# A fused stack of conditional layers on one core: shared weights at another byte remainder, and routed down products as six matmuls of 256 columns

## What is computed

```python
x = x + L0(x, cond_8)     # x @ W0[b].T + bias, W0[b] = sum over g of y[b, g] * weight[g] * mask
x = x + L1(x, cond_8)     # x @ (W_base + 2 * sum over e of w[b, e] * B[e] @ A[e]).T + b_base
x = x + L2(x, cond_8)     # two of 8 experts per sample, weighted by w_route, and one shared expert:
                          #   (gelu(x @ gate) * (x @ up)) @ down, inner width 512
x = x + L3(x, cond_8)     # one of 8 experts per sample: (silu(up) * gate) @ down with biases, inner width 256
```

## Time and profile before

| | |
|---|---|
| median of 3 runs | 135.24 us (135.14 to 135.24) |
| the profiled execution, its own time | 135.81 us |
| its span, first to last instruction | 134.0 us |
| mean granted TensorE clock | 0.996 |
| TensorE busy | 129.9 us, 97% |
| VectorE (DVE), ScalarE (ACT), GpSimd (POOL) busy | 101.7, 99.0, 75.2 us |

### The profile page before, as it was taken

How to read it: one execution, slowest core, us unless ns; L and a number is a source line. 1 busy time by engine, 2 the same in 40 slices (tenths; PEclk the granted TensorE clock), 3 DMA queues, 4 the chain that set the end, 5 groups by cost and what they waited for, 6 DMA issues and landing times.

```text
span 134.0 us, 3164 instructions
## 1 busy us (share of the span) xinstructions
PE 129.9 (97%) x866; PEld 118.9 (89%) x866; DVE 101.7 (76%) x201; ACT 99.0 (74%) x205; POOL 75.2 (56%) x89
## 2 busy tenths in 40 slices
PE   7999999999999999999999999999999999999990
PEld 5988888888888899999999999999999999999980
DVE  0589898797775777768877687877868677898791
ACT  3774699979946478777797777766767659989860
POOL 0228449979980027468496684963452634426770
PEclk9999999999999999999999999999999999999998
DMA  4999999999005955556765657756577465665224
GB/s 151 329 395 400 415 399 402 397 403 378 19 0 213 373 202 232 237 232 247 313 257 224 248 218 313 286 220 248 220 287 312 191 273 227 259 271 203 72 87 157
DMA packets 11489, 34.54 MB, mean 258 GB/s; under 512 B 1104, under 2 KB 2512, under 8 KB 11472
## 3 DMA queue, kind: packets, MB, share of 16 engines
q1 hardware_dynamic: 11184, 34.15, 65.0%
q10 hardware_dynamic: 288, 0.20, 0.5%
HBM read 12.32 MB, written 1.05 MB: 100 GB/s over the span
## 4 chain that ended last, share of the span: by engine, by line
PE 90%; DVE 3%; ACT 1%; POOL 1%; issue 1%; ACTq 0%; DVEq 0%; POOLq 0%
PE up L298 31%; PE acc L298 30%; PE gate L298 29%; DVE x_res L1003 1%; DVE h_pair L923 1%; DVE up L1012 1%; POOL x_lo L779 1%; POOL x_res L805 1%; ACT h_pair L636 0%; ACTq L224 0%; ACT h_act L689 0%; DVE h_pair L1035 0%; DVE acc L1028 0%; ACT h_pair L709 0%; DVE x_res L1044 0%
## 5 line engine op out<-in xcount | busy, mean ns | idle before, releaser
L773 POOL TENSOR_TENSOR dn_lo<-slabs,dn_hi 128x256 fp32r<-128x256 f32 x40 | 29.7, 742 | 39.6 <-ACT dn_hi L654 39.5
L630 ACT ACTIVATE h_act<-gate 128x512 f32<-128x512 f32 x48 | 28.8, 600 | 23.9 <-PE gate L298 22.6
L923 DVE TENSOR_TENSOR h_pair<-up,h_pair 128x512 fp32r<-128x512 f32 x55 | 37.5, 681 | 0.0
L933 DVE SCALAR_TENSOR_TENSOR up<-h_act,w_route,up 128x512 f32<-128x512 f32 x32 | 24.1, 754 | 15.0 <-PE up L298 14.4
L298 PE MATMUL gate<-x_hi,w_gu 128*128 128x256 f32 x160 | 34.3, 278 | 0.0
L298 PE MATMUL up<-x_hi,w_gu 128*128 128x256 f32 x158 | 33.4, 276 | 0.0
L636 ACT ACTIVATE h_pair<-up 128x512 fp32r<-128x512 f32 x55 | 32.8, 597 | 0.0
L298 PEld LDWEIGHTS gate<-x_hi,w_gu 128*128 128x128 f32 x160 | 27.3, 188 | 0.2
L298 PE MATMUL acc<-h_pair,dn_hi 128*128 128x512 f32 (+1 forms) x76 | 27.2, 373 | 0.0
L298 PEld LDWEIGHTS up<-x_hi,w_gu 128*128 128x128 f32 x158 | 26.8, 188 | 0.0
L298 PE MATMUL gate<-x_lo,w_gu 128*128 128x256 f32 x80 | 22.2, 277 | 0.0
(11 more groups left out here) (128 smaller groups left out, 205.1 us busy)
## 6 DMA issues: line engine op xcount, KB each, us to landing
w_gu<-slabs SPq DMA_DIRECT2D x40, 512.0 KB, 3.0
slabs<-slabs_moe SPq DMA_DIRECT2D x8, 768.0 KB, 13.1
slabs<-slabs_l SPq DMA_DIRECT2D x4, 768.0 KB, 8.5
sh_raw<-slabs_shared SPq DMA_DIRECT2D x2, 384.0 KB, 5.2
x_res<-x_rest SPq DMA_DIRECT2D x1, 768.0 KB, 6.9
outT<-x_res SPq DMA_DIRECT2D x6, 128.0 KB, 1.9
slabs<-second_in SPq DMA_DIRECT2D x1, 320.0 KB, 3.3
slabs<-third_in SPq DMA_DIRECT2D x1, 256.0 KB, 3.8
```

Source lines behind the costliest of these rows:

```text
L630: nc.scalar.activation(h_act[:, u % 2, :], gate_ps[u % 2][:], ACT.Gelu_apprx_tanh).then_inc(act_done, 1)
L773: nc.gpsimd.tensor_tensor(dn_lo[:, q % W_SLOTS, :], slab_cols(at, DOWN_AT, 256), dn_hi[:, q % W_SLOTS, :].bitcast(F32), ALU.subtract).then ...
L923: V.tensor_tensor(h_lo[:, u % H_SLOTS, :], h_of(u), h_hi[:, u % H_SLOTS, :].bitcast(F32), ALU.subtract).then_inc(h_lo_done, 1)
L933: ins = V.scalar_tensor_tensor(h_of(u), h_act[:, k, :], weight, h_of(u), ALU.mult, ALU.mult)
```

## The change

Two things are done. place_sh grows from 24 to 40 elements and place_w (16 elements) goes, so that sh_hi and sh_lo begin 64 bytes later, at remainder 416, and everything from w_gu on stays where it was. And `routed_down` calls `slab_down`: six matmuls of 256 columns that all add to the same 256 columns of acc; `add_halves` and its semaphore go, and `add_acc` takes its place with one addition.

```diff
-        place_sh = sb("place_sh", [P, 24])
+        place_sh = sb("place_sh", [P, 40])
         sh_hi = sb("sh_hi", [P, HALVES * SLAB], F32R)
         sh_lo = sb("sh_lo", [P, HALVES * SLAB], F32R)
-        place_w = sb("place_w", [P, 16])
         w_gu = sb("w_gu", [P, W_SLOTS, 2 * SLAB_GU], F32R)
...
-        d_out, half_added, last_half = sem("d_out"), sem("half_added"), sem("last_half")
+        d_out, last_half = sem("d_out"), sem("last_half")
...
                 if j == 0:
                     acc_bank_free(PAIRS + b)
-                hidden_split(R0 + q)
-                pe.wait_ge(wd_hi_done, q + 1)
-                pe.wait_ge(wd_lo_done, q + 1)
-                slot = (R0 + q) % H_SLOTS
-
-                def both(c, start, stop):
-                    w, h = slice(c * P, (c + 1) * P), slice(c * S, (c + 1) * S)
-                    return mm(acc(b, 512), dn_hi[:, q % W_SLOTS, w], h_pair[:, slot, :, h], start, stop)
-
-                def low(c):
-                    w, h = slice(c * P, (c + 1) * P), slice(c * S, (c + 1) * S)
-                    mm(acc(b, S), dn_lo[:, q % W_SLOTS, w], h_hi[:, slot, h], False, False)
-
-                both(0, j == 0, False)
-                low(0)
-                low(1)
-                both(1, False, j == 3).then_inc(down_done, 1)
-
+                slab_down(R0 + q, q, acc(b, S), j == 0, j == 3)
...
-            def add_halves(b, down):
-
-                at = slice(b * S, (b + 1) * S)
-                dve.wait_ge(down_done, down)
-                V.tensor_tensor(x_res[:, at], acc(b, 512)[:, S:2 * S], x_res[:, at], ALU.add).then_inc(half_added, 1)
-                dve.wait_ge(half_added, b + 1)
-                V.tensor_tensor(x_res[:, at], acc(b, S), x_res[:, at], ALU.add).then_inc(acc_read, 1)
-
...
-                        add_halves(b - 1, R0 + 4 * b)
+                        add_acc(b - 1, S, R0 + 4 * b)
...
-                    add_halves(B - 1, T0)
+                    add_acc(B - 1, S, T0)
```

## The result

The changed kernel takes 138.41 us (median of 6 runs, 137.48 to 138.64) against 135.24 for the kernel before (6 runs, 134.91 to 135.32). The profiled execution took 138.64 us with a span of 136.8. The forecast was 134.3, the range ended at 137.3.

The account below looks back on a forecast made before the run. TensorE, busy 97% of the span and never idle between 53 and 118 us, was taken as the bound. From 135.24 us, -0.86 and -0.11 (sum -0.97) gave 134.3 us; the range holding 8 in 10 was 134.1 to 137.3.

Parts of the forecast that it names:

- The narrow form saves 0.86 us: Routed stage: six narrow matmuls per down product bring 32 units from 2.067 to 2.040 us each, -0.86 us.
- The trace has the new form already: Last stage: it already runs six narrow matmuls through the same function, buffers and remainders, at 2.040 us per unit.
- The mixture of remainders costs 0.11 us: From 45.49 to 53.08 us, alternating remainders 352 and 416 cost TensorE 7.59 instead of 7.48 us; equal ones save 0.11.
- For even ones speaks the one sort of wide matmul at 416: Routed down products: the first wide matmul, 53.08 to 53.31 us, was taken as evidence that wide ones at 416 are even.
- The first rival: Shared stage: wide matmuls at 416 are uneven and cost 0.48 to 0.96 us, giving 134.8 to 135.2 us; chance 0.19.
- The sticking pace: From q = 2 to 127 us: some 650 narrow matmuls stay slow, costing 2.7 us, giving 137.2 us; chance 0.30.
- the second rival: Same as the sticking pace: an even last wide matmul leaves the narrow ones behind it slow, 137.2 us; chance 0.30.
- The tail, which I took to move as a whole: Behind 127 us, where TensorE waits twice for the last hidden values: expected to shift as a whole.
- DVE, the covers, the clock: Routed stage: eight saved DVE additions of 0.41 us worth nothing; TensorE never idle at clock 1.00, other engines keep up.
- No fixed part per matmul: Routed stage: 64 more matmuls cost nothing extra, as 226.7 ns is twice 113.3; the skill's 2.5 ns each would be 0.16 us.
- The other rule drawn on there: Shared weights' move: by the skill, separate SBUF read ports make a weight buffer's place worth nothing, so that term is 0.

Follow-up runs that it names:

- e1: The changed kernel's six narrow matmuls, but with shared weights left at 352 (routed at 416): 134.75 us, ratio 0.9958 to the kernel before.
- e7: Changed kernel with all weights moved to 64 bytes before the moving operands (288 against 352): four runs, 134.49 to 137.25 us.
- e12: The kernel of e7 run again unchanged: twelve runs, six from 134.28 to 134.99 us and six from 137.46 to 138.04 us.
- e4: Changed kernel with all weights moved to the moving operands' remainder, 352: 138.86 us, ratio 1.0266 to the kernel before.
- e8: e1 with every operand 64 bytes further on (moving and shared 416, routed 480): 134.82 us, ratio 0.996 to the kernel before.
- e10: e1 with the shared down products beside q = 0, 1 and 2 as six narrow matmuls each: 137.44 us, ratio 1.013 to the kernel before.

## Why the prediction was wrong, by its own steps

**The narrow form saves 0.86 us:** this term of the sum failed, since it lacked a condition. I took 2.040 us per unit over from the last stage; in the changed kernel it is 2.120, and the routed and last stage grew by 2.02 us. The 0.86 is there only if the stage is entered in step, as in e1, which has 73.33 us against 74.18: 0.85. "The trace has the new form already" was true of shape, buffer and distance, and left out the pace that it was handed.

**The mixture of remainders costs 0.11 us:** wrong. With equal remainders, all at +64, the stretch takes 7.64 us, 0.05 more; with unequal ones and narrow products (e1) 7.59, as before. Nor is it a fixed cost of changing width: with all weights at -64 (e7, e12) the widths change just as often, and it takes 7.50.

**"For even ones speaks the one sort of wide matmul at 416":** this step failed first. A single wide matmul that follows an even narrow one shows how it continues a pace, not the pace that a stream of them has: in the changed kernel the wide one behind the even q = 0 takes 226 ns too, and the next two 236 and 231. Nine take 2.10 us. The first rival priced this at 0.48 to 0.96 us; the shared stage lost 0.70.

**The sticking pace:** the mechanism of the second rival, given 0.30, is what happened. Its price was 2.8 us over an even stage; 76.20 - 73.33 = 2.87. Its trigger was off: I had the last wide matmul even, and it takes 231 ns. What I set against it carried no weight: the tail of the kernel before was even already when TensorE had to wait there, so it didn't show a slow pace ending, and the 60 even matmuls of the last stage showed only that an even pace stays.

**The step that put the time outside the range:** I made the rivals exclude each other, 134.8 to 135.2 for one and 137.2 for the other; the second even had the condition that wide matmuls at 416 are even. In this kernel both follow from the same 64 bytes, and so they came together: 135.24 - 0.86 + 0.70 + 0.05 + 2.87 = 138.0, and less the 0.25 us that the matmuls of the tail became shorter 137.8. Measured was 138.41, by the interval of the ratio 137.7 to 138.4; the remainder lies in start and end, which no run ties to the change. Nothing in the trace spoke for only one of the rivals. The tail, which I took to move as a whole, didn't: its waits are gone.

**DVE, the covers, the clock:** right. TensorE is still busy 65.00 of 65.00 us in the stage at a clock of 1.00, so there was nothing for DVE's saved additions to win.

**No fixed part per matmul:** right. e1 issues 64 more matmuls than the kernel before, and 18 of its narrow ones take the same 2.040 us as nine wide ones of its shared stage. The Trainium skill (TensorE: Matmul & The Clock Gate, Back-to-back issue gap) gives N/2.4 + 2.5 ns as the gap of an isolated warm matmul; by that 18 narrow ones would take 22.5 ns more than nine wide ones, and the trace doesn't agree. The other rule drawn on there, that weight loads and the moving operand have ports of their own and take nothing from each other, would make the place of the weights worth nothing, and for the float32r matmuls of this case it isn't: e4 runs the last stage of e1 with the weights at another distance, and has 2.16 us for 2.04.

What the pace is made of stays open. That it depends on the distance between the weights and the moving operand suggests that the two reads meet somewhere; that they do, and where, no run shows.

## What to carry to other kernels

When TensorE is never idle, read the starts of its matmuls, not their durations: here the layout and the pace handed over cost 3 to 6% of every one while TensorE's busy share stayed at 100%. Before taking a pace from one stage for another, look at what enters the stage, since it may be handed down; and when two rivals rest on one cause, price them together. Of the versions tried the fastest median is that of the one that changes only the down products and leaves the shared weights at 352: 134.75 us, 0.4% below the kernel before, with e8, which is the same kernel 64 bytes further on, equal to it at 134.82.

## What the runs showed of the hardware that was not expected

- The paces that repeat themselves fit a grid of 6.67 ns: 113.3, 120.0, 226.7 and 233.3 ns are 17, 18, 34 and 35 times that. Means over all routed units lie on it too: 2.0400, 2.0667, 2.1000, 2.1200 and 2.1600 us are 306, 310, 315, 318 and 324 times, though single matmuls in them need not (117.8 ns). At the granted 2.4 GHz 6.67 ns are 16 periods of the clock. Distance +128 has no such value: its units vary from 2.13 to 2.14 us.
- 64 bytes between the remainders of two buffers decide over 6.7 ns per matmul of 256 columns (120.0 at distance 0, 113.3 at +64 when entered in step) and as much per one of 512 (226.7 at 0, 233.3 at +64).
- A pace can last for over 650 matmuls and through changes of buffer, of PSUM bank and of layer (e10). In these traces narrow matmuls changed from one form to the other only behind a wide matmul or, from even to slow, behind a wait (the tail of e12). A slow pace that ended behind a wait was not seen; in the tail of the kernel before it was even before the wait and is so again behind it.
